# The loads of x are called one tile ahead in three loops of an attention and feed-forward kernel on eight cores

## The reference, cut to what matters

```python
xn = _layernorm(x, axis=-1)                      # x: (8, 2048, 1024) f32
s  = _L0_attn_ref(xn, Wq, bq, Wk, bk, Wv, bv, ln_g, ln_b, Wo, bo)
g  = _silu(_L0_ffn_ref(xn, w_gate, w_up, w_down))
return x + s * g

# _L0_attn_ref: q = xn@Wq+bq (16 heads of 64), k, v (4 heads of 64), causal softmax,
#               layernorm(out) * ln_g + ln_b, then @ Wo + bo
# _L0_ffn_ref:  fp4_linear(silu(fp4_linear(x, w_gate)) * fp4_linear(x, w_up), w_down)
#               fp4_linear quantises both operands to FP4 in blocks of 16 and multiplies in f32
```

## Time and profile before

| | us |
|---|---|
| median of the two timed runs | 7470.22 |
| the two timed runs | 7407.44 and 7532.99 |
| the profiled execution | 7123.81 |
| its span on the slowest core (core 1) | 7122.3 |
| spans of the 8 cores | 7098.6 to 7122.3 |
| TensorE matmul busy in the span | 3945.0 (55%) |
| VectorE busy | 2938.0 (41%) |
| ScalarE busy | 798.3 (11%) |
| GpSimd busy | 289.5 (4%) |

### The profile page before, as it was taken

One profiled execution on the slowest core, in us unless ns is written; L12 is line 12 of the kernel. 1 busy time (PEld: TensorE's weight loads), 2 busy tenths in 40 slices (PEclk: granted clock), 3 DMA queues, 4 the chain that ended last, 5 costly groups with the idle time before them and its releaser, 6 DMA issues.

```text
span 7122.3 us, 35881 instructions; the slowest of 8 cores (7098.6 to 7122.3 us)
## 1 busy us (share of the span) xinstructions
PE 3945.0 (55%) x10160; PEld 1765.9 (25%) x10160; DVE 2938.0 (41%) x7271; ACT 798.3 (11%) x1294; POOL 289.5 (4%) x420
## 2 busy tenths in 40 slices
PE   2600000000757756685776568857756688667746
PEld 1300000000323332322333223223332222223322
DVE  1188888888153550015355100053660000236530
ACT  1100000000210000032000002320000033300000
POOL 0000000000100000010000000100000000000000
PEclk9755555555978878797888779978878799888877
DMA  3111111111112101200111120011101200012101
GB/s 98 36 47 47 41 56 39 55 49 38 30 36 71 48 20 41 75 0 27 56 48 36 41 75 9 0 36 55 64 18 43 75 0 0 9 50 71 36 27 58
DMA packets 140128, 296.00 MB, mean 42 GB/s; under 512 B 10016, under 2 KB 77728, under 8 KB 139936
## 3 DMA queue, kind: packets, MB, share of 16 engines
q0 software_dynamic: 52480, 207.63, 8.8%
q1 hardware_dynamic: 87456, 86.08, 4.0%
HBM read 250.70 MB, written 42.99 MB: 41 GB/s over the span
## 4 chain that ended last, share of the span: by engine, by line
PE 45%; DVE 28%; DMA 9%; DVEq 6%; ACT 5%; issue 4%; ACTq 1%; POOL 1%; PEldq 0%; SPq 0%; PEld 0%; POOLq 0%
PE p L990 10%; PE p L944 6%; DVEq L83 6%; PE p L951 5%; PE p L703 5%; DMA ffnw<-wdq_s 4%; PE p L711 4%; DMA xbuf<-x 3%; PE p L848 3%; PE p L615 3%; PE p L651 3%; DVE qfm L280 3%; PE p L335 3%; DVE qfm L285 2%; PE p L383 2%
## 5 line engine op out<-in xcount | busy, mean ns | idle before, releaser
L944 PE MATMUL p<-ffnw,xnfm 128*128 128x512 f32 (+1 forms) x1536 | 719.1, 628 | 504.7 <-DMA ffnw<-wuq_s 315.5
L990 PE MATMUL p<-hqfm,ffnw 128*128 128x512 f32 x1408 | 677.7, 645 | 334.2 <-DMA ffnw<-wdq_s 334.2
L335 PE MATMUL p<-ident,hqfm 128*128 128x128 f32 (+1 forms) x592 | 133.8, 402 | 1302.8 <-DVE hqfm L306 1295.9
L951 PE MATMUL p<-ffnw,xnfm 128*128 128x512 f32 (+1 forms) x1536 | 620.2, 557 | 0.0
L718 DVE COPY ftmp<-p 65x512 f32<-65x512 f32 x32 | 22.0, 687 | 1387.5 <-PE p L711 1387.5
L944 PEld LDWEIGHTS p<-ffnw,xnfm 128*128 128x128 f32 x1536 | 329.9, 218 | 875.3 <-issue 864.6
L990 PEld LDWEIGHTS p<-hqfm,ffnw 128*128 128x128 f32 x1408 | 290.2, 209 | 720.0 <-issue 720.0
L335 PEld LDWEIGHTS p<-ident,hqfm 128*128 128x128 f32 (+1 forms) x592 | 103.5, 213 | 1333.8 <-issue 1328.7
L703 PE MATMUL p<-probs,vT 128*65 128x512 f32 x640 | 349.5, 698 | 151.6 <-ACT hqfm L689 77.8
L1003 DVE TENSOR_TENSOR sfm<-ftmp,sfm 128x512 f32<-128x512 f32 x32 | 22.1, 692 | 993.9 <-ACTq L83 993.9
L951 PEld LDWEIGHTS p<-ffnw,xnfm 128*128 128x128 f32 x1536 | 291.8, 190 | 312.7 <-issue 306.1
(11 more groups left out here) (154 smaller groups left out, 4907.8 us busy)
## 6 DMA issues: line engine op xcount, KB each, us to landing
ffnw<-wdq_s POOLq DMA_DIRECT2D x32, 1408.0 KB, 8.6
xbuf<-x SPq DMA_DIRECT2D x80, 512.0 KB, 4.0
ffnw<-wgq_s POOLq DMA_DIRECT2D x20, 2048.0 KB, 9.5
ffnw<-wuq_s POOLq DMA_DIRECT2D x20, 2048.0 KB, 14.0
ffnw<-Wq SPq DMA_DIRECT2D x32, 512.0 KB, 5.4
ffnw<-Wo SPq DMA_DIRECT2D x32, 512.0 KB, 4.3
hqfm<-wg POOLq DMA_DIRECT2D x22, 512.0 KB, 5.1
hqfm<-wu POOLq DMA_DIRECT2D x22, 512.0 KB, 4.8
```

The costliest lines, as they stand in the source:

```text
L335: E.do("tensor", lambda e, s=s, pb=pb, j=j, bp=bp, rows=rows: e.transpose(pb[:, j * rows:(j + 1) * rows], s, ident[bp:bp + rows, bp:bp + r ...
L944: E.do("tensor", lambda e, pg=pg, kc=kc, qt=qt, hw=hw: e.matmul(pg[:, 0:hw], xnfm[:, kc * 512 + qt * 128: kc * 512 + qt * 128 + 128], ffnw ...
L951: E.do("tensor", lambda e, pu=pu, kc=kc, qt=qt, hw=hw: e.matmul(pu[:, 0:hw], xnfm[:, kc * 512 + qt * 128: kc * 512 + qt * 128 + 128], ffnw ...
L990: E.do("tensor", lambda e, pd=pd, hc=hc: e.matmul(pd[:, 0:512], wdbuf[:, hc * 128:(hc + 1) * 128], hqfm[:, hc * 512:(hc + 1) * 512], start ...
```

## The change

In the three loops the call of `load_x` for tile tt+1 is put ahead of the work on tile tt. P2 carries the prefetch over the borders of its chunks; A and F begin each chunk with the load of its first tile and stop prefetching at its last. The two halves of `xbuf` are used as before, and each tile is loaded as often as before. The calls in P1 and D are left as they are.

```diff
@@ P2
         for tc in range(NQC):
             E.mark(f"P2.t{tc}")
+            if tc == 0:
+                nxt = load_x(0, 0)
             for ttl in range(4):
                 tt = tc * 4 + ttl
-                xa, qs = load_x(tt, tt % 2)
+                xa, qs = nxt
+                if tt + 1 < NTT:
+                    nxt = load_x(tt + 1, (tt + 1) % 2)
                 E.wait("scalar", qs)
@@ A
             E.mark(f"A{qc}")
+            nxt = load_x(qc * 4, 0)
             for ttl in range(4):
                 tt = qc * 4 + ttl
-                xa, qs = load_x(tt, tt % 2)
+                xa, qs = nxt
+                if ttl < 3:
+                    nxt = load_x(tt + 1, (ttl + 1) % 2)
                 E.wait("scalar", qs)
```

## The result

The changed kernel took 7188.96 us in the median of 11 runs (7038 to 7416), the kernel before 7371.72 us in the median of 10 (7126 to 7533). Executions of one kernel come at two levels, the upper some per cent longer whatever the kernel, and both are in both lists, so the medians say little: the ratio of those at the lower level is 0.9872, with a 95% interval of 0.9837 to 0.9907. That is a gain of 1.3% (0.9 to 1.6%), within the 2% that count as no change. The profiled execution took 7051.34 us against 7123.81 (-72.5 us); core 1, the slowest of before, went from 7122.3 to 7040.9 us (-81.4 us). By the ratio the gain is 91 us of 7124, with 66 to 116 us.

The account below looks back on a forecast made before the run. No single bound: each stage has its own, and only x-load waits can be won back. 20.8 + 2.6 + 5.5 + 18.2 + 40.8 - 2 = 86 us off the 7470 us median gave 7385 us, range 7030 to 7480.

Parts of the forecast that it names:

- P2: P2's tile loop: gaps shrink to those of D's loop without loads, 20.8 us, plus 2.6 us for faster first tiles.
- A0: First A stage: tile 2's load no longer stands behind the `wdq_s` store, so tile 3 starts 5.5 us earlier.
- A1 to A3: Later A stages: three gaps each shrink to those of D's loop without loads, 18.2 us saved.
- F: Four F stages: first add to last tile's first add takes 9.9 us each, 40.8 us saved in all.
- Heads: Start of P2 and each A: two x loads issued back to back cost 0.5 us each, 2 us in all.
- `xbuf` waits: Sign: engines' waits for x loads fall from 428.8 to about 200 us, nearly all in P1 and D.
- loads do not pace the tiles: Rival for P2, A and F: loads landing in 8.8 us pace the tiles, only 40 us saved, 7430 us; chance 0.12.
- The clock did not rise with the denser transposes: Rival for P2 and A: denser transposes raise the TensorE clock, 119 us saved in all, 7351 us; chance 0.10.
- The clock of the dense stages did not fall: Rival for the dense stages: granted clock falls, each per cent costs 32 us, 7512 us at 4%; chance 0.07.
- The estimate of 3.2 us for a load: By the skill page a 512 KB load lands in 3.2 us, making the sum some 5 us better.
- its 8.7 us: F's lower bound from first add to last tile's first add, if neither load is late.
- the 1 in 7: Chance given that a new measurement falls at the profiled level, 346 us under the median, or between.

Follow-up runs that it names:

- the run with more bytes: An extra 256 KB load right before every x load in P2 and A: core 1 7078.4 us on the changed kernel, 7149.8 us on the kernel before.
- the run with the held-back loads: Changed kernel with F's four x loads put into the attention buffer, issued once the third block's down weights landed: core 1 7071.0 us, slowest core 7076 us.

## Why the prediction was right

Step by step, on core 1.

- P2: 23.4 us forecast, 21.7 measured. The pattern of the earlier trace rows held to 0.1 us; of the 2.6 us for a faster first tile only 0.8 came, as one group in three had it.
- A0: 5.5 forecast, 6.6 measured, less 0.2 to 1.8 us behind it on the three cores where Wq came late. The 0.5 us left for that was too small for core 7.
- A1 to A3: 18.2 forecast, 17.8 measured.
- F: 40.8 forecast, 39.3 measured to the end of the last add. The argument that two of three waits shrink and one vanishes is in the rows above. The landing of tile 2's load, the 5.0 us on which it rested, was 4.7 us in F0 of the changed kernel's core 1. The term that was too small is tile 3's load: in F1 it was issued at 4163.76 and its adds began at 4169.85 us, 6.1 us later, so that F takes 10.3 us from the first add to the last tile's first one, for the 9.9 forecast.
- Heads: 2 us of loss forecast; on core 1 2.0 us were lost at P2's and 0.6 gained at the three of A. In the mean of the eight cores it is 1.3 lost at P2's, where the second load is not the cause, and 2.0 at the three of A, where the prefetch is.
- `xbuf` waits: about 200 us forecast as a sign, 256.4 measured. The tile loops are as forecast; the sign left out that the first tiles of P2 and of A1 to A3 and A0's tile 3 still wait, 69.5 us.
- The sum of these is 84 us, the span fell by 81.4; the rest of the kernel took 2.6 us more.

That 86, 84 and 81.4 us agree so well is in part luck of the core. The forecast was worked out from core 1, the slowest of before and the one on which the loops took longest. The same loops gave 78.7 us in the mean of the eight cores and the spans fell by 69.8; the slowest core, which is the time that counts, fell by 72.5, below the prediction's lower bound of 75. The mechanism holds on every core; its size is that of one core.

The rivals: loads do not pace the tiles, by the run with more bytes. The clock did not rise with the denser transposes: behind the first tiles they took 1.94 us in the new pace of 3.66 us, as in D, and the mean of all of them is 416 ns for 412 before (pages, line 335 on `otmp`). By the rule that the prediction weighed, that activity releases the throttle (the Trainium skill, "TensorE: Matmul & The Clock Gate", part 1), the denser loop could have been released; here it was not. The clock of the dense stages did not fall with the change: E's stretches on core 1 sum to 2053.8 us for 2052.8 before. The mean clock of core 1 went from 0.779 to 0.784; 0.003 of that comes from the 81 us that are gone, if they stood at 0.50 as D's tiles did (an estimate).

The estimate of 3.2 us for a load, which the prediction took from the Trainium skill, "DMA: Bandwidth & Descriptors", section "Anatomy of one DMA", was not met. The page gives its fit for DMAs that GpSimd issues, and SP issues these; they landed in 3.8 to 7.8 us, 4.2 in the median, and F came to its 8.7 us only in the runs with no load in it.

The predicted time of 7385 us was carried from a median of two runs; the later median of 7189 lies inside the range only because that reached down to the profiled level. The difference was worked out well, and the level was not known: that the time came out inside the range is owed to the 1 in 7 that the prediction gave to a lower level, not to its sum.

## What to carry to other kernels

Price a prefetch by the second wait, not by the first: find a place in the same trace where the loop runs without loads, and take the difference of the gaps. Then ask at which moment the freed load will be issued and what is issued there: moving F's loads out of F cost more at the down weights than it saved, and swapping a load and a store only changed who was late. A wait on DMA is worth removing only where no other engine is due at the same time, which D shows in the run with all loads early.

## What the runs showed of the hardware that was not expected

The clock has a level in between in dense matmuls. Three windows over P2's third group in the run with all loads early, then the changed kernel's (columns: engines busy, granted clock, DMA share, GB/s):

```profile
189.20:197.80 8.60, 8.60 (x16) 3.40 (x16) 0.00 (x0) 0.00 (x0) 0.00 (x0) 0.81 0.00 0
198.80:207.40 8.60, 8.60 (x16) 3.38 (x16) 0.00 (x0) 0.00 (x0) 0.00 (x0) 0.81 0.00 0
208.40:217.00 8.60, 8.60 (x16) 3.37 (x16) 0.00 (x0) 0.00 (x0) 0.00 (x0) 0.81 0.00 0
```

```profile
189.50:197.00 7.50, 6.57 (x16) 2.88 (x16) 0.00 (x0) 0.69 (x1) 0.00 (x0) 1.00 0.00 0
```

The same 16 matmuls took 8.66 us at a granted 0.81 and 7.11 us at 1.00, with no transfer beside them. In B0 of the run with more bytes on the changed kernel seven of the eight groups took 8.66 us, too. It hit single stretches of some executions, and it goes with differences of tens of microseconds in a core's span: core 1 of the run with the held-back loads, at a mean clock of 0.770, took 7071.0 us, 30 us more than the changed kernel's at 0.784, though its stages in the table add up to 5.8 us less. The Trainium skill, "TensorE: Matmul & The Clock Gate", section "Seeing it yourself", names a peak-current limiter that takes a die to 13/16 once three of its cores run dense matmuls; 0.81 agrees with that number, but here it came and went in stages where all eight cores do the same: in and just behind the changed kernel's B0 every core was granted 0.99 or 1.00 from 1776 to 1830 us, and at that place in the run with more bytes four cores 0.81 from 1795 to 1850 us. What sets it off is not shown. A change of 80 us is therefore read from the gaps of its stage, and only then from the span.
